# Message bias, ScalarE order, a mask and the last relu moved in a two-layer graph kernel

## The reference

```
h  = relu(layernorm(x))
# layer 0, residual
c  = relu(bn1(conv1x1(h)));  xc = relu(bn2(conv17(c)) + h)     # over the 128 nodes
s  = h @ w_se.T + b_se;      A  = exp(-|s_n - s_m|^2) * adj
m  = relu(h @ w_msg.T + b_msg);  nmp = A @ m
r, z, n = gates([xc, nmp], h)                                   # a GRU cell
x  = x + (1 - z) * n + z * h
# layer 1, residual
h2 = relu(layernorm(x))
out = x + adj @ (h2 @ weight) + bias
```

## Time and profile before

| | |
|---|---|
| median of 3 runs | 335.67 us (334.25 to 337.16) |
| the profiled execution | 333.4 us |
| its span | 331.6 us |
| TensorE busy | 320.7 us, 97% |
| VectorE, ScalarE, GpSimd busy | 259.7, 224.0, 145.2 us |
| granted TensorE clock, mean | 1.000 |

### The profile page before, as it was taken

One profiled execution on the slowest core, in us unless ns is written; L12 is line 12 of the kernel. 1 busy time (PEld: TensorE's weight loads), 2 busy tenths in 40 slices (PEclk: granted clock), 3 DMA queues, 4 the chain that ended last, 5 costly groups with the idle time before them and its releaser, 6 DMA issues.

```text
span 331.6 us, 6233 instructions
## 1 busy us (share of the span) xinstructions
PE 320.7 (97%) x2148; PEld 289.4 (87%) x2148; DVE 259.7 (78%) x746; ACT 224.0 (68%) x434; POOL 145.2 (44%) x128
## 2 busy tenths in 40 slices
PE   8699999999999999999999999999999999999995
PEld 5578797988889998899989998899989998899884
DVE  5688999899679977789678987799687867673475
ACT  2799668776758776696776786687776764443453
POOL 7130252139801694119901496018911396038033
PEclk9999999999999999999999999999999999999999
DMA  7902000001300121001300031001200000000003
GB/s 242 352 4 95 3 0 0 3 2 63 127 2 3 32 99 62 2 1 65 127 3 0 18 111 65 0 0 36 97 0 0 2 34 32 1 2 0 1 3 127
DMA packets 7951, 15.02 MB, mean 45 GB/s; under 512 B 1008, under 2 KB 1648, under 8 KB 7792
## 3 DMA queue, kind: packets, MB, share of 16 engines
q1 hardware_dynamic: 7776, 14.62, 12.6%
q10 hardware_dynamic: 144, 0.01, 0.0%
HBM read 10.43 MB, written 4.19 MB: 44 GB/s over the span
## 4 chain that ended last, share of the span: by engine, by line
PE 76%; DVE 13%; ACT 4%; issue 2%; DMA 2%; POOL 1%; SPq 1%; DVEq 0%
PE pQ L327 6%; PE pQ L329 5%; PE pQ L328 5%; PE pP L327 5%; PE pP L329 5%; PE pP L328 5%; PE pNR L327 4%; PE pNR L328 4%; PE pNR L329 4%; PE pF L447 3%; PE pNR L421 3%; DMA bias<-bias_in 2%; PE pI L327 2%; PE pI L329 2%; PE pI L328 2%
## 5 line engine op out<-in xcount | busy, mean ns | idle before, releaser
L1426 POOL TENSOR_TENSOR rs<-ve,neg_half 128x4 f32<-128x4 f32 x15 | 18.3, 1220 | 131.5 <-DVE ve L1190 131.5
L327 PE MATMUL pP<-cx_hi,conv_hi 128*128 128x256 f32 (+1 forms) x179 | 53.7, 300 | 0.0
L329 PE MATMUL pP<-cx_hi,conv_lo 128*128 128x256 f32 (+1 forms) x179 | 51.4, 287 | 0.0
L328 PE MATMUL pP<-cx_lo,conv_hi 128*128 128x256 f32 (+1 forms) x179 | 51.4, 287 | 0.0
L327 PE MATMUL pQ<-cx_hi,conv_hi 128*128 128x256 f32 (+1 forms) x139 | 41.5, 298 | 0.2 <-DVE base L1218 0.2
L329 PE MATMUL pQ<-cx_hi,conv_lo 128*128 128x256 f32 (+1 forms) x139 | 39.7, 285 | 0.0
L328 PE MATMUL pQ<-cx_lo,conv_hi 128*128 128x256 f32 (+1 forms) x139 | 39.6, 285 | 0.0
L327 PEld LDWEIGHTS pP<-cx_hi,conv_hi 128*128 128x128 f32 x179 | 34.0, 190 | 0.5
L328 PEld LDWEIGHTS pP<-cx_lo,conv_hi 128*128 128x128 f32 x179 | 33.8, 189 | 0.5
L329 PEld LDWEIGHTS pP<-cx_hi,conv_lo 128*128 128x128 f32 x179 | 33.7, 188 | 0.4
L792 ACT ACTIVATE work<-work,nb,rs 128x128 f32<-128x128 f32 x60 | 24.6, 483 | 5.6 <-DVE nb L1194 4.8
(11 more groups left out here) (281 smaller groups left out, 963.9 us busy)
## 6 DMA issues: line engine op xcount, KB each, us to landing
x_ring<-x_in SPq DMA_DIRECT2D x16, 256.0 KB, 2.6
adj_ring<-adj_in SPq DMA_DIRECT2D x16, 256.0 KB, 2.8
out<-x_ring SPq DMA_DIRECT2D x15, 256.0 KB, 2.0
work<-conv_in SPq DMA_DIRECT2D x1, 1088.0 KB, 7.2
x_ring<-gate_in SPq DMA_DIRECT2D x1, 576.0 KB, 7.3
out<-x_ring SPq DMA_DIRECT2D x2, 128.0 KB, 1.7
early<-early_in SPq DMA_DIRECT2D x1, 129.5 KB, 3.1
late<-late_in SPq DMA_DIRECT2D x1, 128.0 KB, 7.7
```

Source lines behind the costliest of these rows:

```text
L327: pe.matmul(acc, w_hi, m_hi, start=start, stop=False)
L328: pe.matmul(acc, w_hi, m_lo, start=False, stop=False)
L329: return pe.matmul(acc, w_lo, m_hi, start=False, stop=stop)
L1426: pool.tensor_tensor(rs2[g % 2][:], ve2[g % 2][:], neg_half[:, 0:GG], ALU.pow).then_inc(rs2_set, 1)
```

## The change

Four edits. The bias is loaded ahead of the conv weights. On ScalarE the opening's order becomes `hidden_hi(0)`, `hidden_hi(1)`, `place_bias(0)`, `hidden_graphs(0)`, both conv1 outputs, and then `round_w(0)`; on VectorE `split_w(0)` goes behind `less_odd`. In step 1 alone `masked(b)` goes ahead of `shift1`. The last group's relu is worked out another way: VectorE writes the maximum of zero and x less its mean (`last_centred`), and this is multiplied by the reciprocal deviation, by ScalarE for graphs 0 to 2 and by VectorE for graph 3 (`last_scaled`); `end_pass(1)` also waits for the latter, and GpSimd's two waits for the shifts are gone.

```diff
@@ sync
-            sp.dma_start(conv[:, 0:TAPS * D], conv_in).then_inc(conv_loaded, 16)
             sp.dma_start(bias[:], bias_in).then_inc(bias_loaded, 16)
+            sp.dma_start(conv[:, 0:TAPS * D], conv_in).then_inc(conv_loaded, 16)
@@ tensor, end_pass(1)
                     have(pe, h2_set, END + 1)
+                    pe.wait_ge(h2_last, 1)
@@ scalar, opening
                 hidden_hi(0)
+                hidden_hi(1)
                 place_bias(0)
-                hidden_hi(1)
+                hidden_graphs(0)
+                conv1_out(0)
+                conv1_out(1)
                 act.wait_ge(conv_loaded, 16)
                 round_w(0)
-                conv1_out(0)
-                conv1_out(1)
-                hidden_graphs(0)
                 split_hi_first(0)
@@ scalar, ending
-                have(act, l1_done, END - 1)
-                for j in range(GG):
-                    if j % 2 == 0:
-                        act.wait_ge(nb2_set, END + 1 + j // 2)
-                    last = act.activation(graph(h2[END % 2], j), graph(x1[END % 2], j), ACT.Relu,
-                                          bias=nb2[END % 2][:, j:j + 1], scale=rs2[END % 2][:, j:j + 1])
+                for j in range(GG - 1):
+                    act.wait_ge(centred, j + 1)
+                    act.wait_ge(rs2_set, END + 1 + j // 2)
+                    last = act.activation(graph(h2[END % 2], j), graph(h2[END % 2], j), ACT.Copy, scale=rs2[END % 2][:, j:j + 1])
@@ vector, opening
                 hidden_lo(1)
-                split_w(0)
                 sum_odd()
                 less_odd()
+                split_w(0)
                 split_lo_first(0)
@@ vector, step
+                if t == 1:
+                    masked(b)
                 if t + 2 < NS:
                     shift1([2 * t + 4, 2 * t + 5])
                 if front:
-                    masked(b)
+                    if t > 1:
+                        masked(b)
                     sums_lo(a)
@@ vector, ending (last_stats(e) and last_mean(e) are the two parts of normalise2_half(e))
+            def last_centred(j):
+                have(dve, l1_done, END - 1)
+                dve.tensor_scalar(graph(h2[END % 2], j), graph(x1[END % 2], j), mv2[END % 2][:, j, 0:1], 0.0,
+                                  ALU.subtract, ALU.max).then_inc(centred, 1)
+
+            def last_scaled(j):
+                dve.wait_ge(centred, j + 1)
+                dve.wait_ge(rs2_set, END + 1 + j // 2)
+                dve.tensor_scalar(graph(h2[END % 2], j), graph(h2[END % 2], j), rs2[END % 2][:, j:j + 1], None,
+                                  ALU.mult).then_inc(h2_last, 1)
...
                 residual(END)
-                normalise2_half(0)
-                normalise2_half(1)
-                shift2_half(0)
+                last_stats(0)
+                last_mean(0)
+                last_stats(1)
+                last_centred(0)
+                last_mean(1)
+                last_centred(1)
+                last_centred(2)
+                last_centred(3)
+                last_scaled(3)
                 finish(END - 3)
-                shift2_half(1)
                 finish(END - 2)
                 finish(p)
@@ gpsimd, ending
                 scale2_half(0)
-                pool.wait_ge(nb2_set, END + 1)
                 scale2_half(1)
-                pool.wait_ge(nb2_set, END + 2)
                 with_bias(END)
```

More of the change, by code:

```diff
@@ L152, in gnn_kernel @@
             sem, ("st1_set", "mv1_set", "ve1_set", "rs1_set", "nb1_set", "hn_set"))
-        hn_half = sem("hn_half")
+        hn_half, centred, h2_last = sem("hn_half"), sem("centred"), sem("h2_last")
         hT_placed, hhi_set, hG_set, hT_set, hlo_set = map(sem, ("hT_placed", "hhi_set", "hG_set", "hT_set", "hlo_set"))
@@ L289, in _ @@
             sp.dma_start(early[:], early_in).then_inc(early_loaded, 16)
+            sp.dma_start(bias[:], bias_in).then_inc(bias_loaded, 16)
             sp.dma_start(conv[:, 0:TAPS * D], conv_in).then_inc(conv_loaded, 16)
-            sp.dma_start(bias[:], bias_in).then_inc(bias_loaded, 16)
             load_x(2)
@@ L1356, in step, with last_stats @@
                     gates(t)
-            def normalise2_half(e):
+            def last_stats(e):
                 have(dve, x1_set, END + 1)
-                mv, ve = mv2[END % 2], ve2[END % 2]
                 for j in (2 * e, 2 * e + 1):
@@ L1364, in normalise2_half, with last_mean @@
                 last.then_inc(st2_set, 1)
+            def last_mean(e):
+                mv, ve = mv2[END % 2], ve2[END % 2]
                 dve.wait_ge(st2_set, END + 1 + e)
```

## The result

The changed kernel takes 332.45 us (median of 6 runs, 332.01 to 333.25) where the kernel before takes 335.02 on the same chip (6 runs, 334.25 to 337.16). The ratio is 0.992, 95% interval 0.989 to 0.9949: 2.6 us faster. The forecast was 334.7 with a range from 333.0, so the time lies outside it. The profiled execution after takes 332.01 us with a span of 330.2; the one before took 333.4 with 331.6. Between the two profiles the difference is 1.4 us, between the medians it is 2.6, and the forecast was 1.0 for both. That there are two answers is the first thing to explain. (A ratio in this document is the recorded one of the two sets of runs, with its 95% interval; it can differ by 0.001 from the quotient of the two medians.)

A forecast was written before the change was run, and what follows sets the result against it. TensorE was taken as busy from 85 to 323 us, leaving gains only in gaps before and after. Terms -0.97 - 0.60 + 0.6 = -1.0 us took the median from 335.67 to 334.7, range 333.0 to 336.5.

The forecast's parts named there:

- the last one of the sum: From profile to median: the runs' median, 335.67, is 2.3 us above the profiled time; the same difference gives 334.7.
- The sum itself, -1.0: Whole kernel: opening, mask and ending terms, -0.97 - 0.60 + 0.6, take the profiled time from 333.4 to 332.4 us.
- Rival (4): Opening: TensorE idles 1 us more ahead of the taps, its clock falls to 1.2 GHz; about +5, 340 us; chance 0.03.
- The opening, -0.97: Opening: hidden_hi(1) no longer waits behind place_bias(0) for the bias, so rows_turn(0) comes earlier; -0.97 us, bounds 0 and -1.0.
- None of it released by TensorE or a load: Opening: rows_turn(0)'s pairs follow VectorE's queue from group statistics and a GpSimd power, so 24.18 becomes about 23.2.
- Rival (2): Opening: gives nothing, as an operand on VectorE's way to rows_turn(0) stands still; sum 0, 335.7 us; chance 0.12.
- The mask, -0.60: Step 1: the mask runs while the shift is held, so neighbour_sums(5) moves from 83.56 to 82.96; -0.60 us.
- rival (3): Step 1: the later shift is held through a second GpSimd instruction; +0.9 not -0.6, sum +0.5, 336.2 us; chance 0.09.
- The last relu, +0.6: Ending: the held scaling delays end_pass(1), and finish and stores queue behind it; +0.6 us, bounds -0.28 and +0.9.
- Its deciding step: Ending: GpSimd's with_bias(END) gets in first, 1.27 us, and holds VectorE's scaling to 327.2; end_pass(1) +0.36 us.
- Rival (1): Ending: the scaling is not held by GpSimd; ending -0.28, sum -1.85, 333.8 us; chance 0.25.

## Why the prediction was wrong

**The failed step is the last one of the sum**: "The median of the runs shown is 335.67, 2.3 above the profiled one ...; the same difference on it gives 334.7." The sum itself, -1.0 on the profiled 333.4, gives 332.4, and the changed kernel's median is 332.45. The 2.3 us were not scatter that any kernel has, but for the most part (1.7 to 2.0 us) a fall of the clock in the opening in most executions of the kernel before (71 of 83 runs), and it went with the two gaps. The sign that was there to see: the profiled execution lay under the lowest of the three runs shown (334.25), and a deviation of one sign and that size wants a cause before it is carried over. Without it the difference is 332.45 against 333.1, the median of the 12 runs at full clock, or against the 333.4 of the kernel with both gaps filled: 0.65 to 1.0 us where the sum was 1.0, though from different chips. That the sum taken from the profile, 332.4, meets the median so closely is partly luck: the profile of before had the long power, which the sum did not touch, and the ending cost 0.2 more than its term.

**Rival (4) had the mechanism on the wrong kernel.** It asked whether the changed kernel's longer idle ahead of the taps would lower the clock, and read the earlier trace rows as proof that the clock is safe at 11.40 to 13.70. That row shows one execution. The gaps that matter are those which the change closes, ahead of conv1(1) (0.96 us in the earlier trace rows) and ahead of the messages. The Trainium skill, TensorE: Matmul & The Clock Gate, "Part 1: The HAM clock gate", says that the gate's window is free-running, and that the number of slow products at the start of a kernel is therefore "run-variable". Here the clock falls after it had risen, and the three levels in the runs of one unchanged kernel show that this varies from run to run as well.

**The opening, -0.97**: right to 0.05 us at each step up to `split_lo_first(0)`, and at `rows_turn(0)` 0.86 more. The mechanism was right; that the times agree so closely is partly chance, since the same steps come 0.2 us later in the profile of opening and mask (conv1(1) at 10.66). "None of it released by TensorE or a load" held in this profile; where the clock falls it doesn't, and in the kernel before, run again, VectorE waited 0.39 us for messages(1) and TensorE came to `rows_turn(0)` without a wait. Missed was that the power's 2.77 us were 1.67 and a delay: five of the six later powers of 128x8 in the same trace take 1.65 us each (the sixth 2.01). Rival (2) fell.

**The mask, -0.60**: measured 0.55 to 0.6 in the traces, 1.1 in the medians of the mask alone with an interval from 0.6 to 2.1. The shift was issued and held as forecast; rival (3) fell. (The unheld length was read from a row of 128x2 elements; the row of 22.72 above shows that 0.17 us holds for 128x8 too.)

**The last relu, +0.6**: measured +0.78 in the trace. Its deciding step, that GpSimd gets in first and holds the scaling, was right; the wait on `h2_last` that removes the clash proves the cause. Rival (1) fell. Two sizes were off and nearly cancel. The `last_centred` stand 0.20 us apart, not 0.29 (0.67 for three), so that VectorE's queue behind the scaling reached the last addition at 327.01, 0.22 later relative to before, not 0.48. The stores cost more than I allowed: their issues take 0.46 us in place of 0.33 and stand 0.51 us apart behind the 1.53 us of the three before, so the last one is issued at 327.67, 0.24 after its addition ends where it was 0.03 before, and from there to the end of the span it takes 330.2 - 327.67 = 2.53 us where it took 331.6 - 329.42 = 2.18. That is 0.21 + 0.35 = 0.56 us, beside the 0.1 that I took and above its bound of 0.4; 0.22 + 0.56 is the 0.78.

**What is left open**: which idle, where and how long, brings the clock down. The clocks show that filling one of two gaps lowers the share of fallen runs from 71 of 83 (16 of 22 on the same chip) to 3 or 4 of 10, and that a single longer gap behind the messages brought it in one run of four. Also open is which of two instructions released within 0.2 us of each other gets the port in the opening, and how often each does: no run's time is tied to it but the profiled ones.

## What to carry to other kernels

When the profiled execution and the median of the runs lie apart by more than the change is expected to give, find out first what state the profile missed: compare each run's mean clock, and put idle products into TensorE's gaps as a test that moves nothing else. Where VectorE and GpSimd are released by the same instruction, say who goes first: a wait on GpSimd of 0.5 us turned a held 1.21 us into 0.29 and gave back 0.9 us in the trace (1.2 between medians, 332.45 and 331.2, from two chips). An operation whose length differs from that of its twins in the same trace is in part a wait.

## What the runs showed of the hardware

- TensorE's clock in the first 20 us of a one-core kernel falls in some executions and not in others of the same program: the runs of the unchanged kernel have mean clocks near 1.00, 0.994 and 0.99 and medians of 333.1, 334.5 and 335.6 us (12, 31 and 40 runs).
- A tensor_scalar with a per-partition scalar from memory, SBUF to SBUF, is held by a large GpSimd tensor_tensor as one with constants is: 1.21 us in place of 0.29.
- The port works both ways: a VectorE instruction with two SBUF operands (128x1024) lengthens a 128x8 GpSimd power in some executions from 1.67 to 2.77 us, while it is itself no slower (1.22 us against 1.25); put first, it does so too (2.57 us).
